# A decoder layer's cross-attention: key banks, a maximum in PSUM, pairs on GpSimd, and a context product split into rounded parts

## The reference, cut to what matters

```python
q = (hidden_states @ Wq).reshape(B, Sq, H, D)
k = (encoder_hidden_states @ Wk).reshape(B, Skv, H, D)
v = (encoder_hidden_states @ Wv).reshape(B, Skv, H, D)
q = rmsnorm(q, gq)
k = rmsnorm(k, gk)
scores = jnp.einsum('bqhd,bkhd->bhqk', q, k) * scale
attn = jax.nn.softmax(scores, axis=-1)
out = jnp.einsum('bhqk,bkhd->bqhd', attn, v)
return out.reshape(B, Sq, H * D) @ Wo
```

## Time and profile before

| what | value |
|---|---|
| median of 3 runs | 1399.74 us (1399.17 to 1405.49) |
| the profiled execution | 1401.35 us, span 1399.5 us |
| TensorE busy | 1354.1 us, 97% |
| VectorE busy | 1220.2 us, 87% |
| GpSimd busy | 1104.4 us, 79% |
| ScalarE busy | 911.7 us, 65% |
| weight loads (PEld) | 1023.8 us, 73% |
| granted TensorE clock, mean | 0.986 of full |

### The profile page before, as it was taken

One profiled execution on the slowest core, in us unless ns is written; L12 is line 12 of the kernel. 1 busy time (PEld: TensorE's weight loads), 2 busy tenths in 40 slices (PEclk: granted clock), 3 DMA queues, 4 the chain that ended last, 5 costly groups with the idle time before them and its releaser, 6 DMA issues. The chain is left out here.

```text
span 1399.5 us, 23607 instructions
## 1 busy us (share of the span) xinstructions
PE 1354.1 (97%) x6366; PEld 1023.8 (73%) x6366; DVE 1220.2 (87%) x1785; ACT 911.7 (65%) x2726; POOL 1104.4 (79%) x991
## 2 busy tenths in 40 slices
PE   7799799999999999999999999999999999999978
PEld 4678678777777777777777777777777777767658
DVE  5779789999998899988998999999889999997675
ACT  2645477777777777777777777777777777742342
POOL 3700013999999999999999999999999999985140
PEclk9899999999999999999999999999999999999989
DMA  7040010001010100000010101010101000020200
GB/s 240 32 161 1 25 45 9 14 12 34 9 37 14 33 17 28 21 25 23 21 27 18 28 16 30 16 31 14 33 12 36 9 22 1 23 91 1 62 1 27
DMA packets 17922, 45.52 MB, mean 33 GB/s; under 512 B 1600, under 2 KB 11968, under 8 KB 17040
## 3 DMA queue, kind: packets, MB, share of 16 engines
q1 hardware_dynamic: 17088, 44.24, 9.7%
q10 hardware_dynamic: 720, 0.10, 0.0%
HBM read 40.41 MB, written 3.93 MB: 32 GB/s over the span
## 5 line engine op out<-in xcount | busy, mean ns | idle before, releaser
L977 POOL TENSOR_TENSOR xa_scores<-xa_scores,xa_gmax 125x448 f32<-125x448 f32 x352 | 455.3, 1297 | 13.9 <-DVE xa_scores L1116 13.9
L1147 PE MATMUL xa_k_ps<-wk_parts,xa_ctxT_hi 128*125 128x512 f32 x768 | 436.9, 569 | 4.9 <-DVE wk_parts L1140 4.9
L888 POOL TENSOR_TENSOR xa_den<-probs,xa_den 125x448 f32<-125x448 f32 x311 | 414.2, 1332 | 26.1 <-ACT probs L1037 12.6
L1214 PE MATMUL xa_o_ps<-probs,xa_ctx_nat 125*128 125x448 f32 x768 | 351.9, 539 | 0.0
L1101 DVE TENSOR_TENSOR xa_cmax<-xa_scores,xa_cmax 125x448 f32<-125x448 f32 x320 | 340.3, 1063 | 0.7
L1090 DVE TENSOR_REDUCE xa_ss<-xa_sq 125x6 f32<-125x768 f32 x360 | 338.1, 939 | 0.0
L1016 ACT ACTIVATE xa_k_ps<-xa_k_ps 125x128 f32<-125x128 f32 x720 | 190.1, 264 | 189.7 <-PE xa_k_ps L1149 140.6
L1149 PE MATMUL xa_k_ps<-wk_parts,xa_ctxT_lo 128*125 128x512 f32 x768 | 304.2, 396 | 0.0
L1148 PE MATMUL xa_k_ps<-wk_parts,xa_ctxT_hi 128*125 128x512 f32 x768 | 303.9, 396 | 0.0
L1018 ACT ACTIVATE xa_sq<-xa_k_ps 125x768 f32<-125x768 f32 x360 | 288.0, 800 | 0.0
L1075 DVE TENSOR_TENSOR xa_scores<-xa_s_ps,xa_rk 125x448 f32<-125x448 f32 x384 | 236.5, 616 | 56.7 <-PE xa_s_ps L1149 47.1
(11 more groups left out here) (163 smaller groups left out, 1653.8 us busy)
## 6 DMA issues: line engine op xcount, KB each, us to landing
ctxT_in<-in_ctxT SPq DMA_DIRECT2D x16, 750.0 KB, 10.8
xa_ctx_nat<-in_ctx SPq DMA_DIRECT2D x16, 750.0 KB
qo<-in_xq_w SPq DMA_DIRECT2D x1, 2048.0 KB, 11.1
qo<-in_xo_w SPq DMA_DIRECT2D x1, 2048.0 KB, 20.7
vo_scratch<-qo SPq DMA_DIRECT2D x2, 1024.0 KB, 4.2
vo<-vo_scratch SPq DMA_DIRECT2D x1, 2048.0 KB, 8.1
xq_wkT<-in_xk_wT SPq DMA_DIRECT2D x4, 256.0 KB, 4.1
probs<-in_xk_w SPq DMA_DIRECT2D x1, 1024.0 KB, 8.8
```

What stands on the lines that cost most here:

```text
L888: eng.tensor_tensor(den[:, hy, :], probs[0:KP, y % NPR, :], den[:, hy, :], ALU.add).then_inc(den_done, 1)
L977: pool.tensor_tensor(score_slot(y), score_slot(y), gmax[:, (y // KT) % 2, :], ALU.subtract).then_inc(shift_done, 1)
L1147: pe.matmul(out, l_hi, r_hi, start=True, stop=False)
L1214: pe.matmul(o_ps[:, hy, 0:UW], ctx_nat[:, of.parity(), ty, :], probs[0:KP, y % NPR, :], start=(ty == 0), stop=(ty == KT - 1)).then_inc(pv_ ...
```

## The change

- Keys: three PSUM banks in turn in place of two pairs; squares are taken bank by bank, so ScalarE handles 512 columns, and later in the step the other 512.
- The running maximum lies in the freed PSUM bank (`max_ps`); the last one of a half goes to SBUF for the turn.
- GpSimd shifts two tiles in one instruction, and adds two tiles at a time into `den2`; a `fold` in step 4 of the next half adds its two parts into `den`. The adds move one step back, the closing from step 6 to 8.
- ScalarE takes the exponential of two tiles in one instruction, in odd steps.
- Every odd tile's product with the context is `three`: ScalarE takes its exponential a second time, rounded (`p_hi`), VectorE makes `p_lo`, in even steps; the odd tiles of the context are split once a phase in two parts (`nat_hi` by ScalarE in steps 8 and 12, the rest by GpSimd one step later).
- The denominator: ScalarE rounds `den` in step 6, GpSimd makes `den_lo` in step 7, TensorE multiplies both with ones in step 8, two F32R matmuls. In the last phase it stays float32.
- The transposed context is loaded in six parts, over the place of the tiles just used; its lo parts lie over its input. w1 is loaded one phase later, after the last scores.

The diff, cut:

```diff
-DEN_LAG = EXP_LAG + 1
+DEN_LAG = EXP_LAG + 2
+FOLD_LAG = DEN_LAG + 1
+LOW_LAG = EXP_LAG + 1
+NAT_SPLITS = (8, 12)
+ADDS = KT // 2
 PV_LAG = EXP_LAG + 3
-TD = 6
+TD = 8
+TD_LAST = 6
...
+def splits_den(ph, j):
+
+    return j >= 0 and ph.b != B and j % KT == TD - 2 and closes(ph, j + 2)
...
+def vector_shifts(ph):
+
+    return ph.b == B
...
-        k_ps = ctx.enter_context(nc.psum_tensor("xa_k_ps", [P, 2, 2, 512], F32))
+        k_ps = ctx.enter_context(nc.psum_tensor("xa_k_ps", [P, 3, 512], F32))
+        max_ps = ctx.enter_context(nc.psum_tensor("xa_max_ps", [P, 512], F32))
...
+            def load_part(ph, c):
+
+                sp.wait_ge(s_done, pos_s(ph, KT + 2 * c + 1) + 1)
+                to = ph.shift(2)
+                src = a.ctxT[to.b] if to.b is not None else a.ctxT[bass.ds(to.at(1, 0), 1)].rearrange("o c k -> (o c) k")
+                sp.dma_start(ctxT_in[:, to.parity(), 2 * c:2 * c + 2, :].rearrange("c t p -> c (t p)"),
+                             src[:, 2 * c * KP:(2 * c + 2) * KP]).then_inc(part_loaded[to.parity()][c], 16)
...
-                    y = lagged(ph, j, SHIFT_LAG)
-                    if y is not None and not vector_shifts(ph, y):
+                    y = lagged_pair(ph, j, SHIFT_LAG)
+                    if y is not None and not vector_shifts(ph):
                         if y % KT == 0:
                             pool.wait_ge(gmax_ready, ph.at(2, y // KT + 1))
-                        if ph.b == B - 1:
-                            pool.wait_ge(shift_done, ph.at(STEPS, y))
-                        pool.tensor_tensor(score_slot(y), score_slot(y), gmax[:, (y // KT) % 2, :],
-                                           ALU.subtract).then_inc(shift_done, 1)
-                    y = lagged(ph, j, DEN_LAG)
-                    if y is not None and y % KT and not vector_adds(ph, y):
-                        add_den(pool, ph, y)
+                        pool.tensor_tensor(score_pair(y), score_pair(y), gmax_pair(y), ALU.subtract
+                                           ).then_inc(shift_done, 2)
+                    y = lagged_pair(ph, j, DEN_LAG)
+                    if y is not None and y % KT:
+                        wait(pool, exp_done, ph.at(STEPS, y + 2))
+                        if y % KT == 2:
+                            wait(pool, den_done, ph.at(2 * ADDS, ADDS * (y // KT)))
+                            so_far = probs_pair(y - 2)
+                        else:
+                            wait(pool, den_done, ph.at(2 * ADDS, ADDS * (y // KT) + y % KT // 2 - 1))
+                            so_far = den2[:, :, :]
+                        pool.tensor_tensor(den2[:, :, :], probs_pair(y), so_far, ALU.add).then_inc(den_done, 1)
+                    y = lagged_pair(ph, j, FOLD_LAG)
+                    if y is not None and y % KT == KT - 2:
+                        before = Phase(ph.b, ph.pair, ph.i) if h else ph.shift(-1)
+                        if before.b is None or 2 * before.b + 1 - h >= 2:
+                            wait(pool, s_done, pos_d(before, 1 - h) + 1)
+                        wait(pool, den_done, ph.at(2 * ADDS, ADDS * (y // KT + 1) - 1))
+                        pool.tensor_tensor(den[:, :], den2[:, 0, :], den2[:, 1, :], ALU.add).then_inc(den_done, 1)
...
+                    if splits_den(ph, j - 1):
+                        pool.wait_ge(den_hi_ready, ph.at(2, h - 1))
+                        pool.tensor_tensor(den_lo[:, :], den[:, :], den_hi[:, :].bitcast(F32), ALU.subtract
+                                           ).then_inc(den_lo_ready, 1)
...
-                        wait(act, k_done, ph.at(STEPS, STEPS + j + 1))
+                        wait(act, k_done, ph.at(2 * STEPS, 2 * STEPS + 2 * j + 1))
                         wait(act, summed, ph.at(STEPS, STEPS + j - 1))
...
+                        act.activation(squares(ph, j)[:, 0:4 * XD], k_ps[0:KP, (2 * j) % 3, :], ACT.Square
                                        ).then_inc(squared, 1)
...
-                    y = lagged(ph, j, EXP_LAG)
+                    y = lagged_pair(ph, j, EXP_LAG)
                     if y is not None:
-                        wait(act, shift_done, ph.at(STEPS, y + 1))
-                        wait(act, pv_done, ph.at(STEPS, y - NPR + 1))
-                        wait(act, den_done, ph.at(STEPS, y - NPR + 1))
-                        act.activation(probs[0:KP, y % NPR, :], score_slot(y), ACT.Exp).then_inc(exp_done, 1)
+                        wait(act, shift_done, ph.at(STEPS, y + 2))
+                        wait(act, pv_done, ph.at(STEPS, y - NPR + 2))
+                        if ph.b is None or STEPS * ph.b + y >= NPR:
+                            wait(act, den_done, adds_done(ph, y - NPR))
+                        act.activation(probs_pair(y), score_pair(y), ACT.Exp).then_inc(exp_done, 2)
+                        act.activation(p_hi[:, y // 2 % (NPR // 2), :], score_slot(y + 1), ACT.Exp
+                                       ).then_inc(p_hi_ready, 1)
+                    if j in NAT_SPLITS and ph.within(0, 15):
+                        part = NAT_SPLITS.index(j)
+                        act.wait_ge(nat_loaded[ph.parity()], nat_loads(ph))
+                        act.activation(nat_hi[:, ph.parity(), 3 * part:3 * part + 3, :], odd_tiles(ctx_nat, ph, part),
+                                       ACT.Copy).then_inc(nat_hi_ready, 1)
+                    if ph.within(-1, 14):
+                        own = vector_heads(ph) - 4
+                        act.wait_ge(k_done, ph.at(2 * STEPS, 2 * STEPS + 2 * j + 2))
+                        for g in range(own, 4):
+                            head = UH * (j % 2) + 4 + g
+                            cols = k_ps[0:KP, (2 * j + 1) % 3, g * XD:(g + 1) * XD]
+                            act.activation(cols, cols, ACT.Square, accum_out=ss[:, j // 2, head:head + 1])
+                        act.activation(squares(ph, j)[:, 4 * XD:(4 + own) * XD],
+                                       k_ps[0:KP, (2 * j + 1) % 3, 0:own * XD], ACT.Square).then_inc(squared, 1)
+                    if splits_den(ph, j):
+                        act.wait_ge(den_done, ph.at(2 * ADDS, ADDS * (h - 1)))
+                        act.activation(den_hi[:, :], den[:, :], ACT.Copy).then_inc(den_hi_ready, 1)
...
-                        if t == 1:
-                            wait(dve, max_turned, ph.at(2, h - 1))
-                            dve.tensor_tensor(cmax[0:KP, h, :], score_slot(j), score_slot(j - 1), ALU.max
-                                              ).then_inc(max_done, 1)
-                        else:
-                            wait(dve, max_done, ph.at(2 * (KT - 1), (KT - 1) * h + t - 1))
-                            dve.tensor_tensor(cmax[0:KP, h, :], score_slot(j), cmax[0:KP, h, :], ALU.max
-                                              ).then_inc(max_done, 1)
+                        wait(dve, max_done, ph.at(2 * (KT - 1), (KT - 1) * h + t - 1))
+                        so_far = score_slot(j - 1) if t == 1 else max_ps[0:KP, 0:UW]
+                        if t == KT - 1:
+                            wait(dve, max_turned, ph.at(2, h))
+                        dve.tensor_tensor(cmax[0:KP, :] if t == KT - 1 else max_ps[0:KP, 0:UW], score_slot(j),
+                                          so_far, ALU.max).then_inc(max_done, 1)
...
+                    y = lagged_pair(ph, j, LOW_LAG)
+                    if y is not None:
+                        dve.wait_ge(p_hi_ready, ph.at(KT, y // 2 + 1))
+                        dve.tensor_tensor(p_lo[:, y // 2 % (NPR // 2), :], probs[0:KP, (y + 1) % NPR, :],
+                                          p_hi[:, y // 2 % (NPR // 2), :].bitcast(F32), ALU.subtract
+                                          ).then_inc(p_lo_ready, 1)
...
-                        wait(pe, squared, ph.at(STEPS, STEPS + j - 1))
-                        project_k(ph, j, 0)
+                        wait(pe, squared, ph.at(2 * STEPS, 2 * STEPS + 2 * j - 2))
+                        project_k(ph, j, 0).then_inc(k_done, 1)
...
-                        pe.wait_ge(den_done, ph.at(STEPS, KT * (h - 1)))
+                        out = s_ps[:, bank_d(ph, h), 0:UW]
                         wait(pe, s_taken, pos_d(ph, h) - 1)
-                        pe.matmul(s_ps[:, bank_d(ph, h), 0:UW], ones[:, 0:1].broadcast_to([KP, P]), den[:, h, :],
-                                  start=True, stop=True).then_inc(s_done, 1)
+                        if ph.b == B:
+                            pe.wait_ge(den_done, ph.at(2 * ADDS, ADDS * (h - 1)))
+                            pe.matmul(out, ones[:, 0:1].broadcast_to([KP, P]), den[:, :],
+                                      start=True, stop=True).then_inc(s_done, 1)
+                        else:
+                            pe.wait_ge(den_hi_ready, ph.at(2, h - 1))
+                            pe.matmul(out, ones_r[:, 0:1].broadcast_to([KP, P]), den_hi[:, :], start=True, stop=False)
```

(17 more changed lines are left out.)

133 lines of the change are left out of this document (72 added, 61 removed).

## The result

| | before | after |
|---|---|---|
| median of 4 runs each, side by side | 1400.02 us (1399.17 to 1405.49) | 1481.85 us (1480.86 to 1483.26) |
| ratio, with its 95% interval | | 1.056 (1.053 to 1.060) |
| profiled execution; its span | 1401.35; 1399.5 us | 1481.17; 1479.2 us |

The kernel is slower by 82 us, where 55 was forecast. The time lies in the stated range, but above the forecast's own stretch (1430 to 1480), at the lower end of the one given to rival B.

The account below looks back on a forecast made before the run. TensorE was taken as the bound before; after the change, its 33.58 us half plus a 3.0 wait for den_lo, with 0.2 for VectorE, made 36.8. Halves +57.7, ends -3.7, on 1401.35: 1455 us, range 1390 to 1515.

Parts of the forecast that it names:

- rival B: VectorE becomes the bound through waits at p_lo and the mean: half 38.4 us, total 1500 us, chance 0.26.
- From the maximum (gmax) on ... 17.1: GpSimd's ordered work from gmax to den_lo: 15.95 us, with three p_lo holds of 0.38 each 17.1 us.
- It waits 3.0 us in every half: TensorE reaches the denominator at 700.4, den_lo is ready at 703.4; the 3.0 us wait is not made up.
- That is the same delay, not another: Part of the denominator's wait shows earlier, at the key product behind ScalarE's squares, and is no additional delay.
- The sum. 28 halves x (36.8 - 34.74): All 28 regular halves lengthen from 34.74 to 36.8 us, adding 57.7 us.
- Ends. ... the chain has room, -1.2 each: In the last two halves no keys are projected and GpSimd has room: -1.2 us each.
- the tail's -1.3: The tail, paced by TensorE's context and early products, saves 1.3 us over nine tiles.
- w: VectorE's wait for GpSimd at each two-operand p_lo: near 0.7 us; VectorE's sum per half is 29.4 + 8w.
- the refining: GpSimd's refining between the first shift and the next add on the way to den_lo: 1.67 us.
- GpSimd idle before the first shift of a half: A sign that would show the forecast's mechanism: GpSimd idle there in each half; no size given.
- A: TensorE stays the bound if den_lo's path is 14.1 us or less: 1365 us, chance 0.13.
- C: Between: den_lo's path 14.6 to 15.7 us, half 34.1 to 35.2, total 1380 to 1410 us, chance 0.11.

Follow-up runs that it names:

- den32: The kernel after, with the denominator as one float32 matmul, without den_hi and den_lo: 1442.32 us, 1.028 of the kernel before.
- floatpv: The kernel after, with all context products float32, without p_hi, p_lo and the split of the context: 1396.30 us, 0.996 of the kernel before.
- unlocked: The kernel after, with a VectorE maximum reading one SBUF operand in place of p_lo after the first three pairs: 1407.07 us, 1.004 of the kernel before.
- noplo: The kernel after, with p_lo made for the first three pairs alone, all matmuls kept: 1409.59 us, 1.006 of the kernel before.
- laterefine: The kernel after, with GpSimd refining the keys' factor two steps later, behind the second shift: 1525.54 us, 1.089 of the kernel before.

## Why the prediction was right or wrong

- **The mechanism held in the order of time, and in part in the cause.** "From the maximum (gmax) on ... 17.1": measured 17.1, in the mean of 26 halves. "It waits 3.0 us in every half": 1.65 + 1.71 in the half shown, in step 4 and step 8. The first was forecast behind the second shift and shows behind the first, and "That is the same delay, not another" doesn't hold: without den_lo (den32) step 4 still takes 3.94 us. The half of 36.8: 36.83 in the 21 halves away from the loop's turn. Pairs "at 2.09, or 2.47 with a wait": 2089 and 2473 ns are the least and the largest of the shifts; p_lo "from 0.61 to 2.6": 607 to 2594 ns.
- **Failed step one: "The sum. 28 halves x (36.8 - 34.74)".** It has every half alike. Five of the 26 hold the loop's turn and took 39.8 us; together the 26 gave +69.1 instead of 26 x 2.06 = 53.6, that is 15.5 of the 26 us by which the sum was short. Part of it is clock: its mean over each of these five halves is 0.92 to 0.96. The kernel before took 34.7 in these halves too: VectorE's idle time was 1.2 to 1.6 us there and hidden. floatpv, without p_lo, pays 1.1 us at a turn, unlocked 1.6, the kernel after 3.0. The trace of before shows this idle time, mostly as "issue", and I read past it.
- **Failed step two: "Ends. ... the chain has room, -1.2 each" and the tail's -1.3.** Behind the thirtieth half's start +8.0 was measured where -1.6 was forecast (2.06 for one regular half, then the ends): 9.6 of the 26 us. The last half did as forecast (29.85 us to its last score, 30.88 before). The one ahead of it, from 1306.3, took 34.85 us, 31.60 before. The 17.7 busy of 32 is GpSimd's in the last half, while VectorE takes most shifts of phase 15, and the change, by its own list, gives these back to GpSimd. In the half from 1306.3 it is busy for 31.7 of 34.9 us, in the same half before for 24.7 of 31, and TensorE waits 3.5 us for den_lo once (kernel after, then before):

```profile
1306.30:1341.20 34.90, 29.52 (x126) 23.52 (x125) 25.19 (x37) 13.44 (x27) 31.70 (x21) 0.95 0.17 61
```

```profile
1232.00:1263.00 31.00, 28.61 (x116) 20.71 (x115) 30.62 (x40) 10.80 (x24) 24.74 (x22) 1.00 0.28 102
```

  In noplo GpSimd has these shifts too, and that half takes 31.5; so it took both, the shifts and p_lo. In the tail the products behind the last score took 36.0 us, not 32.4 less 1.3; without p_lo it is 31.2, and p_lo comes there behind VectorE's own shifts. That the load of w1 costs nothing held: from the start of the last product to the end are 72.1 us, 72.5 before.
- **Mis-sized: w.** "w is near 0.7" and a mean of p_lo "near 1.3": measured 1.523, and 1.523 - 0.61 = 0.91, nearer to rival B's 1.0. And its weight: the prediction put p_lo into the path with three holds of 0.38, and else at 0.2. Without the contention the half falls to 34.87, by 2.5 us. 1.0 of it is the path (17.1 to 16.1); the rest is gmax, whose end comes 1.4 us earlier in the half, because VectorE isn't behind. The sum gave most of the wait to GpSimd's list and hit the regular half all the same (36.8), which is partly luck; the two are one loop, in which each holds the other.
- **Mis-sized: the refining.** It stands in the 15.95 with its whole 1.67 us. It took 2.0 us, but began 0.8 before gmax was there, so only 1.2 lay on the path (1.16 in the half shown). The sign "GpSimd idle before the first shift of a half" failed with it: 4.2 us in the whole span. An estimate of the prediction's sum with 1.16 in place of 1.67 is a half of about 36.3; longer pairs (2.13 and 2.51 where 2.05 was taken) made up for it, by luck.
- **Rivals.** A (a path of 14.1 us or less) fell: it is 17.1, and none in the table is under 15.1. floatpv shows the side it spoke for: with p_lo out, TensorE is the bound again. B (VectorE the bound, a half of 38.4, 1500 us) was nearly right in w and wrong in the rest: VectorE has 757 of 830 us and itself waits, the regular half is 36.83, and the instruction of the mean (L1180), which B had wait for a whole pair, takes 0.45 us on average. C (a path of 14.6 to 15.7) fell with A.
- **GpSimd's pair.** The Trainium skill's estimate of 1.87 us (GPSIMD Engine Reference, section 2.1 Instruction dispatch) isn't reached by any of 142 shifts: 2.09 is the least. The row's slope of 2.1 ns a column is the page's 2.5 cycles at 1.2 GHz; what the estimate leaves out is a fixed part of about 0.2 us (2.09 - 896 x 2.1 ns), which the prediction's 2.09 holds.

## What to carry to other kernels

Before an instruction with two SBUF operands is put on VectorE, ask whom it will meet on GpSimd: 0.61 us of work cost up to 2.59 here, and probably most where it stands between a maximum and whoever waits for it. An operation that is saved on a full engine and made on one with 10% free isn't a gain when both lie on one loop of waits; take the order of time over one whole turn of the program's loop, not over one pattern. And read of each end of the kernel which engine the change gives its work to, before its busy share is taken as room.

## What the runs showed that I had not expected

- The loop's turn leaves VectorE and ScalarE idle for 1 to 3 us, every four halves. In the kernel before TensorE doesn't feel it; in the variants of the change, laterefine apart, the fourth half is longer than the mean of the others, by about 1 us or more (35.5 against 34.4 in floatpv).
- After a stop of 2.25 us in a stretch with the clock at full, the granted clock was 0.70 and 0.62 over the next 5 us; in laterefine, with stops of up to 3.1, its mean from 350 to 1230 us is 0.95, and 1.00 in floatpv from 370 to 1200. These waits of TensorE were paid twice, and in laterefine the second payment, of 33 us, was most of the loss.
- Moving den_lo two steps down GpSimd's list made it later by as much as the steps gave (path 17.1 to 22.8).
